# Attention kernel: two of four heads' probabilities turned in 32x32 blocks and through HBM, rows normalised behind the output product

## What is computed

```python
x = x + attn1(lora_linear(x))       # the first stage
h = cond2(x)                        # the part that the change touches
x = x + ffn(h)                      # the last stage

def cond2(x):                       # 32 query heads, 8 groups of keys and values, heads of 128
    q, k, v = rope(rmsnorm(x @ Wq.T)), rope(rmsnorm(x @ Wk.T)), x @ Wv.T
    k_all = concat([paged_k_cache, k])           # 512 cached + 128 new rows
    v_all = concat([paged_v_cache, v])
    scores = where(valid, q @ k_all.T / sqrt(128), -1e30)
    o = softmax(scores) @ v_all                  # per head, 128 x 640 probabilities
    return o.reshape(8, 128, 4096) @ Wo.T
```

## Time and profile before

| | us |
|---|---|
| median of 3 runs | 1362.9 (1361.45 to 1364.13) |
| profiled execution, its span | 1360.4 |
| PE busy | 1317.0 (97%) |
| DVE busy | 1077.3 (79%) |
| ACT busy | 862.2 (63%) |
| POOL busy | 653.2 (48%) |
| mean DMA traffic | 79 GB/s |

### The profile page before, as it was taken

One profiled execution on the slowest core, in us unless ns is written; L12 is line 12 of the kernel. 1 busy time (PEld: TensorE's weight loads), 2 busy tenths in 40 slices (PEclk: granted clock), 3 DMA queues, 4 the chain that ended last, 5 costly groups with the idle time before them and its releaser, 6 DMA issues.

```text
span 1360.4 us, 26524 instructions
## 1 busy us (share of the span) xinstructions
PE 1317.0 (97%) x8104; PEld 1132.6 (83%) x8104; DVE 1077.3 (79%) x2964; ACT 862.2 (63%) x2501; POOL 653.2 (48%) x647
## 2 busy tenths in 40 slices
PE   6899997899999999999999999999999999999998
PEld 4666765688888888888888888888888888888878
DVE  4689777688878887888888888888878888888876
ACT  2677777566766666667666766666666666666651
POOL 0455466443644464436543654465345534554531
PEclk8899998999999999999999999999999999999999
DMA  8444544544121212131223122222212121212121
GB/s 285 149 157 153 158 155 137 151 125 109 32 63 32 79 32 63 34 81 35 55 44 81 35 54 49 68 48 47 65 45 63 32 79 32 63 32 67 34 78 63
DMA packets 196400, 107.59 MB, mean 79 GB/s; under 512 B 140961, under 2 KB 180898, under 8 KB 195106
## 3 DMA queue, kind: packets, MB, share of 16 engines
q1 hardware_dynamic: 195248, 105.71, 28.9%
q10 hardware_dynamic: 1010, 0.17, 0.1%
HBM read 101.66 MB, written 37.75 MB: 102 GB/s over the span
## 4 chain that ended last, share of the span: by engine, by line
PE 90%; DVE 4%; ACT 2%; issue 1%; POOL 1%; DMA 0%; SPq 0%; DVEq 0%; ACTq 0%; POOLq 0%
PE ps L1221 12%; PE ps L1223 12%; PE ps L1222 12%; PE ps L1272 10%; PE ps L1293 5%; PE ps L1286 5%; PE ps L1287 5%; PE ps L1306 4%; PE ps L1312 4%; PE ps L1305 4%; PE ps L247 2%; PE ps L1248 2%; PE ps L259 2%; PE ps L306 1%; PE ps L297 1%
## 5 line engine op out<-in xcount | busy, mean ns | idle before, releaser
L1427 ACT ACTIVATE b_pf<-b_sm,b_nb,b_rstd 128x640 f32<-128x640 f32 x256 | 235.1, 918 | 101.8 <-DVE b_nb L1536 101.7
L1433 ACT ACTIVATE b_p_h<-ps 128x640 fp32r<-128x640 f32 x256 | 180.5, 705 | 180.3 <-PE ps L1272 179.8
L1550 DVE TENSOR_TENSOR b_p_l<-ps,b_p_h 128x640 fp32r<-128x640 f32 x256 | 210.6, 823 | 80.6 <-ACT b_p_h L1433 73.1
L1529 DVE CUSTOM_DVE_ANT_0 b_sm<-ps,mask_row 128x640 f32<-128x640 f32 x256 | 209.0, 816 | 1.4 <-issue 0.4
L1272 PE MATMUL ps<-ident,b_pf 128*128 128x128 f32 x1280 | 181.7, 273 | 4.6 <-DVE b_p_l L1550 3.0
L1545 DVE TENSOR_SCALAR b_pf<-b_pf,b_ri 128x640 f32<-128x640 f32 x256 | 159.4, 623 | 28.1 <-DVE b_ri L1542 0.9
L1221 PE MATMUL ps<-b_w_h,x1t_h 128*128 128x512 f32 (+1 forms) x512 | 179.3, 350 | 0.3 <-DVE b_w_l L1611 0.3
L1221 PE MATMUL ps<-b_kt_h,b_qt_h 128*128 128x320 f32 x512 | 173.7, 339 | 1.5 <-DVE b_mx L1529 1.4
L1222 PE MATMUL ps<-b_w_l,x1t_h 128*128 128x512 f32 (+1 forms) x512 | 173.4, 339 | 0.0
L1223 PE MATMUL ps<-b_w_h,x1t_l 128*128 128x512 f32 (+1 forms) x512 | 172.8, 338 | 0.0
L1272 PEld LDWEIGHTS ps<-ident,b_pf 128*128 128x128 f32 x1280 | 151.9, 140 | 24.7 <-issue 5.3
(11 more groups left out here) (170 smaller groups left out, 3233.1 us busy)
## 6 DMA issues: line engine op xcount, KB each, us to landing
kv_of_batch<-in_kv SPq DMA_DIRECT2D x128, 256.0 KB
b_ck<-kv_of_batch SPq DMA_DIRECT2D x64, 256.0 KB, 3.7
b_cv<-kv_of_batch SPq DMA_DIRECT2D x256, 64.0 KB, 2.2
raw<-in_w SPq DMA_DIRECT2D x32, 384.0 KB, 5.2
raw<-in_wo SPq DMA_DIRECT2D x32, 256.0 KB, 3.8
a_xt<-in_xt SPq DMA_DIRECT2D x8, 256.0 KB, 5.5
a_xin<-in_x SPq DMA_DIRECT2D x8, 256.0 KB, 5.4
x<-a_x SPq DMA_DIRECT2D x8, 256.0 KB, 5.3
```

The costliest lines, as they stand in the source:

```text
L1427: act.activation(pf[:, h % 2], sm[:, h % 2], ACT.Exp, bias=nb[:, m.b % 2, h:h + 1], scale=rstd[:, m.b % 4, h:h + 1], accum_out=rs[:, m.b % ...
L1433: act.activation(p_h[:, :, h * P:(h + 1) * P], turned_row, ACT.Copy).then_inc(ph_sb, 1)
L1529: dve.tensor_tensor_reduce(sm[:, h % 2], score_row, mask_row[:, m.b], 1.0, MASKED, ALU.add, ALU.max, mx[:, k, h:h + 1]).then_inc(mx_sb, 1)
L1550: dve.tensor_tensor(p_l[:, :, cols], turned_row, p_h[:, :, cols], ALU.subtract).then_inc(pl_sb, 1)
```

## The change

Heads 0 and 1 (`BY_DMA`) no longer go through PE and PSUM. DVE turns each 32x32 block of `pf` in place of its quadrant into `blk` (`turn_blocks`), SP writes `blk` to a tensor in HBM (`blocks_away`) and reads it back into `moved` with the blocks placed so that the whole row is turned (`blocks_back`, four DMAs), ACT rounds that to `p_h` (`high_moved`) and POOL writes the rest to `p_l` (`low_moved`). Heads 2 and 3 (`BY_PE`) go as before. Rows are not scaled any more ahead of the turn: the output product is made head by head (`out(m, h)`, heads 0 and 3 in bank SM, 1 and 2 in bank OT), and `accumulate(m, h)` multiplies each by the inverse row sum and adds it to `hacc`. One reciprocal serves four heads. The order in every slot is changed. The scratch reserved for dynamic DMAs is set to 4096.

```diff
+BY_DMA = (0, 1)
+BY_PE = (2, 3)
@@ sync
+            def blocks_away(m, h):
+                d = BY_DMA.index(h)
+                sp.wait_ge(blk_sb, len(BY_DMA) * m.n + d + 1)
+                wait(sp, moved_in[d], 16 * LT * m.n)
+                sp.dma_start(blocks_dram[d], blk[:, d]).then_inc(blk_out[d], 16)
+            def blocks_back(m, h):
+                d = BY_DMA.index(h)
+                sp.wait_ge(blk_out[d], 16 * (m.n + 1))
+                wait(sp, ml_sb, len(BY_DMA) * (m.n - 1) + d + 1)
+                for c in range(LT):
+                    rows_of = blocks_dram[d].rearrange("(a i) (c n) -> c i a n", a=LT, c=LT)[c]
+                    sp.dma_start(moved[c * QUAD:(c + 1) * QUAD, d].rearrange("p (a n) -> p a n", a=LT), rows_of).then_inc(moved_in[d], 16)
             def slot(m, one, two, last):
+                blocks_away(m, 0)
+                blocks_back(m, 0)
+                blocks_away(m, 1)
...
+                    key_rows(two)
+                blocks_back(m, 1)
+                    value_rows(two)
...
@@ tensor
             def values_of_lows(m):
-                pe.wait_ge(pl_sb, REP * (m.n + 1))
+                pe.wait_ge(pl_sb, len(BY_PE) * (m.n + 1))
+                pe.wait_ge(ml_sb, len(BY_DMA) * (m.n + 1))
+            def out(m, h):
+                if h == 0:
...
+                    pe.wait_ge(ol_sb, m.n + 1)
+                    pe.wait_ge(wol_sb, KT * (m.g + 1))
+                    wait(pe, h_sb, REP * m.n)
+                if h == 2:
+                    pe.wait_ge(h_sb, REP * m.n + 2)
+                tile = slice(h * P, (h + 1) * P)
+                three(ps[:, OUT[h], :], (o_h[:, tile], o_l[:, tile]), (wo_h[:, h], wo_l[:, h])).then_inc(wo_ps, 1)
@@ vector
+            def invert(m):
+                dve.wait_ge(exp_sb, REP * (m.n + 1))
+                dve.reciprocal(ri[:, m.b % 2], rs[:, m.b % 2]).then_inc(ri_sb, 1)
+            def turn_blocks(m, h):
+                d = BY_DMA.index(h)
+                if m.n == 0:
+                    dve.wait_ge(x1_out, 16 * B)
                 dve.wait_ge(exp_sb, REP * m.n + h + 1)
-                dve.reciprocal(ri[:, k, h:h + 1], rs[:, k, h:h + 1]).then_inc(ri_sb, 1)
-                dve.tensor_scalar(pf[:, h % 2], pf[:, h % 2], ri[:, k, h:h + 1], None, ALU.mult).then_inc(pn_sb, 1)
+                wait(dve, blk_out[d], 16 * m.n)
+                dve.transpose(by_quadrant(blk[:, d]), by_tile(pf[:, h % 2])).then_inc(blk_sb, 1)
-            def accumulate(m):
-                dve.tensor_tensor(hacc[:, m.b], ps[:, SM, :], hacc[:, m.b], ALU.add).then_inc(h_sb, 1)
+            def accumulate(m, h):
...
+                dve.scalar_tensor_tensor(out=hacc[:, m.b], in0=ps[:, OUT[h], :], scalar=share, in1=hacc[:, m.b],
+                                         op0=ALU.mult, op1=ALU.add).then_inc(h_sb, 1)
```

More of the change, by code:

```diff
@@ L1204, in slot, with rows @@
                         chunk(m.g + 1, c)
+            def rows(m):
+                key_rows(m)
+                value_rows(m)
             def first_out_weights():
@@ L1335, in slot @@
                     turn_rows(pe, 0)
[L1336 to L1341, removed]
                 if last:
-                    out_of_highs(last)
-                if m:
-                    turn_probs(m, 2)
+                    out(last, 0)
+                    out(last, 1)
                 if one:
                     scores(one, 0)
-                if last:
-                    out_of_lows(last)
                 if two:
@@ L1355, in slot @@
                     rest_rows(pe, 0)
+                turn_probs(m, 3)
             tensor_first(pe, (project_q, project_kv, turn_q, turn_new, scores))
             slots(pe, slot)
-            turn_probs(end, 3)
+            out(end.before(), 2)
+            out(end.before(), 3)
             turn_rows(pe, 2)
@@ L1364, in _ @@
             low_rows(pe, 0)
-            out_of_highs(end)
-            out_of_lows(end)
+            for h in range(REP):
+                out(end, h)
             batches(pe)
@@ L1442, in slot @@
             def slot(m, one, two, last):
+                if m.n == 0:
+                    exponent(m, 0)
                 if one:
@@ L1446, in slot @@
                     high(last, 3)
+                    high_moved(last, 1)
+                exponent(m, 1)
                 if m.n == end.n:
@@ L1478, in slot @@
                     squares(two)
-                if m:
-                    high(m, 2)
-                    exponent(m, 3)
-                if m and m.b == 5:
+                if m.b == 5:
                     for c in range(KT):
                         q_weights(m.g + 1, c)
+                if one:
+                    exponent(one, 0)
             scalar_first(act, (q_weights, kv_weights, squares, new_kv, queries, cache_keys, new_keys, cache_values))
@@ L1488, in _ @@
             high(end, 3)
+            high_moved(end, 1)
             h_out(act, 2)
@@ L1620, in _ @@
             slots(dve, slot)
+            accumulate(end.before(), 2)
             low(end, 3)
+            accumulate(end.before(), 3)
             choose(dve, 0)
             h_rest(dve, 2)
+            invert(end)
             output(end)
-            accumulate(end)
+            for h in range(REP):
+                accumulate(end, h)
             rows_dve(dve)
@@ L1703, in _ @@
             slots(pool, slot)
+            low_moved(end, 1)
             pool_ffn(pool)
```

224 lines of the change are left out of this document (124 added, 100 removed).

## The result

The changed kernel takes 1493.4 us (median of 4 runs, 1490.9 to 1495.2) against 1362.6 (4 runs) of the kernel before beside it: ratio 1.0964, 95% interval 1.0951 to 1.0977. The forecast was 1376 with a range of 1338 to 1440: the sign was right, the size was not, and the time lies outside the range. The profiled span is 1493.4 against 1360.4.

The account below looks back on a forecast made before the run. PE was taken to bound the kernel, with loops through DVE/ACT and POOL meeting it at 15.6 us. 1360.4 - 59.5 + 27 + 17.5 + 16 + 10 + 2 = 1373.4; median 2.5 higher: 1376, range 1338 to 1440.

Parts of the forecast that it names:

- What bounds the kernel; PE's saving: All items: PE is the bound; dropping two heads' turns saves 1.08 us an item, 16.73 to 15.65 if PE stays it.
- The loop through DVE and ACT: Ordinary item: a loop over DVE, ACT and PE takes 15.62 us; 15.8 taken, -59.5 us over 64 items.
- the sum of 1373.4: Whole kernel: 1360.4 - 59.5 + 27 + 17.5 + 16 + 10 + 2, in us of profiled span.
- Rival D: On the loop: new DVE or POOL operations slow by 0.3 to 0.7 a piece, about 1440 us; chance 0.15.
- POOL's loop: Ordinary item: PE's `values_of_lows(last)` waits for POOL's `low_moved(last,1)`, ready 6.0 us in, about when PE comes there.
- Unknown costs: New operations: DVE transpose taken as 0.82 us, uncertainty -26 to +155 us; `low_moved`'s strided writes 0 to +64 us.
- The round trip outside group 0: Blocks' store to HBM and return: about 3 us of cover, so no cost outside group 0.
- b = 1: Slot with output weights: PE waits for POOL's last two weights; 19.1 us, +3.4 over 15.8 in 8 slots, +27 us.
- b = 6: Slot behind the query weights: POOL's weights delay `rope_keys` and `low_moved`; +2.5 us in 7 slots, +17.5 us.
- The start: First `turn_blocks` waits for all eight stores of `x`, the last landing at 269 behind gathers: +16 us.
- Group 0: Four slots with gathers: SP's gathers, DMAs, loads and waits take 17 to 20 us against 15.8; +10 us.
- The end: Tail: `out(end,2)` waits some 0.9 us for `accumulate(end,1)`, and POOL has one more operation of 1.6: +2 us.

## Why the prediction was wrong, step by step

**What bounds the kernel; PE's saving: right.** A head's turn by PE was priced at 0.54 us and an item on PE's work alone at 15.65. With both other loops shortened an item takes 15.60 (the busy time of PE, whose ends are modelled, is full at 15.60 and at 15.88 alike, so it doesn't prove that PE sets it).

**The loop through DVE and ACT: the step that failed.** It was named as the second bound at 15.62, with one size in it wrong. The prediction said: "A bias starts 0.93 after its maximum and ends at 1.09; the pair is 1.00 when something follows." Those rows are biases that no operation of POOL held up. With the changed order the pairs of heads 2 and 0 meet one that does and take 1.14 and 0.38 us more. By 64 items the ordinary item cost +36.5 us instead of the forecast -59.5: **96 of the 120 us** by which the span of 1493.4 missed the sum of 1373.4. The mended bias takes 1.40 of the 1.50 us back that an ordinary item was over the forecast (17.30 to 15.90), though only 66 us of the whole, since other waits then came forward. A hint of it stood in the trace of before: the answer on L1536 had a largest duration of 1002 ns beside a median of 158. I looked at two rows of the line and not at its spread. Rival D, a slow new operation, gave 1440 at most for "0.3 to 0.7 a piece"; what was slow was an old one, next to a new neighbour.

**POOL's loop: right in place.** "Three loops meet at 15.6 and none has room": with the bias mended the two loops beside PE's measured 15.89 each, against 15.8 taken.

**Unknown costs.** The transpose lasts 0.84 us and steps by 0.77 (908.35 to the maximum at 909.12): 0.82 and 0.74 were taken. The Trainium skill, "Vector Engine (DVE) Microarchitecture Reference", section 3.8, has it pipelined at one element per cycle and lane, and the trace agrees: it takes about as long as the mask of that shape (0.84 against 0.80). The two rows that the prediction held against it were themselves lengthened beside POOL. The 623 ns of the scaling are the mean of 552 to 1696 (L1545 above), and the 1623 ns of `a_kr` of one at 0.72 us and seven at 1.75:

```profile
L561 DVE TENSOR_TENSOR a_kr<-a_rope_a,a_rope_b x8: 723/1752/1760, 25.7 to 203.8; 128x512 f32<-128x512 f32 x8
```

Each of those seven starts inside an operation of POOL that lasts 1.7 us and ends 0.55 us behind it. So the wait that decided the case stood in the earlier trace rows, and the prediction read it as a possible rate of DVE.

`low_moved` takes 1.57, taken 1.6: the runs of 32 columns cost nothing. The round trip outside group 0 is hidden; store and return land in 2.6 and 2.1 us in the median on the page after, 2.3 and 2.2 were taken.

**b = 1: right place and cause, mis-sized.** Forecast 3.4 us (19.1 less 15.8 is 3.3) over an ordinary item, measured 6.05 (+21 us in eight groups). The 5.5 us of idle were seen for a smaller part, and the clock that fell in them not at all. Putting the weights first takes 5.3 of the 6.05 away.

**b = 6: 2.5 forecast (34.0 less 31.6 is 2.4), 1.45 measured** (-7 us in seven slots). Why it was less isn't shown; the ordinary item beside it was itself held by the bias. With the bias mended it was 4.3 over, then 1.5 when POOL's order was mended too, so the cause named, `low_moved` late behind POOL's queue, was right.

**The start: right at 16.** DVE waited 16.55 us. What was not foreseen is that taking this wait away gains only 3 us, since the gathers then hold the round trip instead. **Group 0: 10 forecast, 14.9 measured. The end: 2 forecast, some 5 measured.**

**The range.** It was built from the sum and a few named mishaps. The steady item had a term whose size hung on which engine is busy next to it, and that term counts 128 times.

## What to carry to other kernels

When an order is changed, read each DVE instruction's largest duration and not just its usual one or its mean, and note which of them have all their tensors in SBUF: here these were the ones that waited for operations of POOL, and a new order or a bound elsewhere makes that visible. For an instruction of one column a per-row scalar as its second operand took the wait away; for one of 640 columns it did not (L1545). When work is taken off the engine that bounds a kernel, price every other loop to a tenth of a microsecond, and before moving an instruction ask who is queued behind it on each engine along the way: here one move of two weights gained 38 us, and a move of four squares lost 48.

## What the runs showed of the hardware

- A 128x1 operation on DVE with two inputs in SBUF takes 0.15 us, or up to 1.31 beside a `TENSOR_TENSOR` of 512 to 1024 columns on POOL; beside POOL's 128x5 power it stays at 0.16. With one input and a per-row scalar it takes 0.20 to 0.22, in all 256 of the run.
- A `TENSOR_SCALAR` on DVE of 128x640 from SBUF to SBUF takes 0.55 us, or up to 1.70 beside POOL, though it has one tensor input. The wait goes the other way too: in the kernel before, 55 of POOL's 64 `cache_values` (128x512) start while such a scaling runs and take 1.56 to 1.60 us, the other nine 1.28 to 1.30.
- A 32x32 block transpose of 128x640 float32 on DVE takes 0.84 us, as long as the mask or a subtraction of that shape.
- PE, idle for 5.5 us, came back at a granted clock of 0.50 for 2.6 us (0.62 over four), with steps of 0.43 us instead of 0.23 for six matmuls of 512 columns.
- Eight gathers of 256 KB, each with its page number read first, take SP 14.6 us to issue, and a 320 KB store behind them on SP is issued only then.
